# A branch hint at the head of each turn of TensorE's cross-attention loop in a decoder block

## What is computed

```python
x = x + _L0_attn_ref(_layernorm(x), wq, wk, wv, wo)        # causal, 32 heads of 16, 8 key/value heads
x = x + _L0_xattn_ref(_layernorm(x), ctx_4096, mask, Wq, Wk, Wv, Wo, q_norm_w, k_norm_w)
x = x + _L0_ffn_ref(_layernorm(x), gate_w, up_w, down_w, fc1_w, fc2_w, expert_w, ln_gamma, ln_beta)
```

```python
q = _rmsnorm((hidden_states @ Wq.T).reshape(bsz, q_len, H, HD).transpose(0, 2, 1, 3), q_norm_w)
k = _rmsnorm(jnp.repeat(k, GROUPS, axis=1), k_norm_w)
scores = jnp.einsum('bhqd,bhkd->bhqk', q, k) * scale + attention_mask[:, :, :, :kv_len]
probs = jax.nn.softmax(scores.astype(jnp.float32), axis=-1)
out = jnp.einsum('bhqk,bhkd->bhqd', probs, v).transpose(0, 2, 1, 3).reshape(bsz, q_len, H * HD)
return out @ Wo.T
```

## Time and profile before

| what | value |
| --- | --- |
| median of 3 runs | 1723.91 us |
| lowest and highest run | 1723.14 and 1726.42 us |
| the profiled execution | 1727.06 us |
| its span (first to last instruction) | 1725.3 us |
| TensorE matmuls busy | 1644.1 us, 95% |
| TensorE weight loads busy | 1340.6 us, 78% |
| DVE, ACT, POOL busy | 66%, 44%, 38% |
| mean granted TensorE clock | 0.989 of full speed |

### The profile page before, as it was taken

One profiled execution on the slowest core, in us unless ns is written; L12 is line 12 of the kernel. 1 busy time (PEld: TensorE's weight loads), 2 busy tenths in 40 slices (PEclk: granted clock), 3 DMA queues, 4 the chain that ended last, 5 costly groups with the idle time before them and its releaser, 6 DMA issues.

```text
span 1725.3 us, 40966 instructions
## 1 busy us (share of the span) xinstructions
PE 1644.1 (95%) x16856; PEld 1340.6 (78%) x16856; DVE 1141.4 (66%) x1977; ACT 764.2 (44%) x1396; POOL 656.1 (38%) x511
## 2 busy tenths in 40 slices
PE   5899999999999999999978999999999999998998
PEld 5566788887888888788865568888788888786897
DVE  4489767576766666774545877666676766758743
ACT  2576445345354444431225755444454453544321
POOL 3496323234233232461125954243232342324600
PEclk9999999999999999999999999999999999999999
DMA  5110012021020110121111101020120210202100
GB/s 169 62 38 7 20 45 63 2 63 45 20 63 8 57 48 23 50 74 38 54 64 53 31 1 47 17 63 20 44 63 1 63 38 27 69 2 62 31 19 25
DMA packets 26215, 73.04 MB, mean 42 GB/s; under 512 B 3120, under 2 KB 3376, under 8 KB 26032
## 3 DMA queue, kind: packets, MB, share of 16 engines
q1 hardware_dynamic: 26032, 70.22, 13.0%
HBM read 66.01 MB, written 4.19 MB: 41 GB/s over the span
## 4 chain that ended last, share of the span: by engine, by line
PE 64%; issue 13%; POOL 10%; DVE 10%; ACT 2%; DMA 1%; POOLq 0%; SPq 0%; DVEq 0%; ACTq 0%
PE acc L407 10%; PE acc L408 9%; PE acc L409 9%; PE y L407 8%; PE y L409 7%; PE y L408 7%; POOL w_lo L1654 5%; PE quad L672 4%; POOL prob L1667 2%; PE quad L701 2%; PE quad L588 2%; POOL prob L1673 2%; DVE pmax L1247 1%; PE y L685 1%; DVE kv L1347 1%
## 5 line engine op out<-in xcount | busy, mean ns | idle before, releaser
L407 PE MATMUL y<-w_hi 128*128 128x512 f32 x576 | 234.5, 407 | 26.1 <-POOL w_lo L1654 16.7
L1658 POOL TENSOR_TENSOR qkrs<-qkve,mhalf 128x10 f32<-128x10 f32 x64 | 124.9, 1952 | 325.6 <-DVE qkve L1339 325.6
L1667 POOL TENSOR_TENSOR prob<-prob,pmax 128x512 f32<-128x512 f32 x128 | 135.9, 1062 | 274.5 <-DVE pmax L1247 274.0
L407 PE MATMUL acc<-w_hi,xn_hi 128*128 128x512 f32 (+1 forms) x576 | 228.7, 397 | 11.2 <-DVE xn_lo L1188 11.2
L408 PE MATMUL y<-w_lo,w_hi 128*128 128x512 f32 x576 | 226.1, 393 | 0.0
L409 PE MATMUL y<-w_hi,w_lo 128*128 128x512 f32 x576 | 226.1, 393 | 0.0
L408 PE MATMUL acc<-w_lo,xn_hi 128*128 128x512 f32 (+1 forms) x576 | 222.4, 386 | 0.0
L409 PE MATMUL acc<-w_hi,xn_lo 128*128 128x512 f32 (+1 forms) x576 | 220.6, 383 | 0.0
L1264 DVE TENSOR_TENSOR x<-y,x 128x512 f32<-128x512 f32 x144 | 99.3, 690 | 168.2 <-PE y L409 168.2
L1654 POOL TENSOR_TENSOR w_lo<-stage,w_hi 128x1024 fp32r<-128x1024 f32 (+1 forms) x88 | 170.7, 1947 | 89.9 <-ACT w_hi L852 89.9
L1673 POOL TENSOR_TENSOR prob<-prob,prec 128x512 f32<-128x512 f32 x128 | 148.3, 1159 | 137.8 <-DVE prec L1255 137.8
(11 more groups left out here) (129 smaller groups left out, 3773.1 us busy)
## 6 DMA issues: line engine op xcount, KB each, us to landing
stage<-in_w_cross SPq DMA_DIRECT2D x64, 512.0 KB, 3.7
stage<-in_w_cross SPq DMA_DIRECT2D x32, 256.0 KB, 3.3
stage<-in_w_ffn SPq DMA_DIRECT2D x16, 512.0 KB, 3.6
x<-in_x SPq DMA_DIRECT2D x8, 512.0 KB, 3.9
stage<-in_w_self SPq DMA_DIRECT2D x8, 512.0 KB, 4.5
kt<-in_ctx SPq DMA_DIRECT2D x16, 256.0 KB, 2.9
out_x<-x SPq DMA_DIRECT2D x16, 256.0 KB, 2.0
stage<-in_w_self SPq DMA_DIRECT2D x4, 256.0 KB, 3.6
```

The lines of the kernel that those rows point to most:

```text
L407: nc.tensor.matmul(target, l_hi, r_hi, start=first, stop=False)
L1658: return nc.gpsimd.tensor_tensor(target, source, mhalf[:, 0:width], ALU.pow)
L1667: nc.gpsimd.tensor_tensor(pr, pr, spread(pmax[:, buffer, :], 8, SEQ), ALU.subtract).then_inc(s_sub.sem, 1)
```

## The change

The loop of TensorE in `cross_attention` is opened with the option that puts a prefetch hint for the loop's closing branch at the head of the body. The hint is the first instruction of every turn and names the branch that closes the turn. The loops of the other engines are left as they are.

```diff
             def cross_attention(half):
-                with pe.Fori(0, NG - 1) as turn:
+                with nc.Fori(0, NG - 1, engines=bass.OrderedEngineSet([pe.engine]), hint_back_edge=True) as turn:
                     for c in range(CHUNKS):
                         slot(Place(2, half, turn), c)
```

## The result

The median went from 1723.53 us (4 runs, 1720.71 to 1726.42) to 1706.49 us (4 runs, 1702.11 to 1708.24): a ratio of 0.9897, 95% interval 0.9872 to 0.9923. That is 17.0 us less, between 13 and 22. The profiled execution has 1707.25 us with a span of 1705.5. Forecast were 1703.8 us, with a range of 1701.5 to 1712.

A forecast was written before the change was run, and what follows sets the result against it. TensorE was taken as the bound, standing at its loop's closing branch until code was read. From the median 1723.9 us, 12 returns gave -20.2, the hint 0 and leaving the loops 0: 1703.8 us, range 1701.5 to 1712.

The forecast's parts named there:

- The bound and the stall: TensorE bounds; at 12 loop returns it waits for its own code at L720, not POOL: 20.2 us, 1.68 a return.
- (a): Head of each of 14 turns: the added hint instruction costs 0, at most 1.1 us if not covered by queued matmuls.
- (b): At the 12 returns: branches under 3.3 us cost nothing, so the loss of 20.2 us goes.
- (c): Slots around a return: no late data takes the stall's place; DVE's w_lo is ready 1.35 us before the matmul is due.
- (d): Outside the loop: nothing changes, the work there follows TensorE, which arrives earlier by the whole sum.
- leaving the loops 0: At the loops' exits: a term of 0 us in the forecast's sum.
- rival 2: Loop's end: hint comes too late, 1712 us; or it displaces the block behind the loop, exits cost 3.4, 1707.2; together 7%.
- The rule that spoke against it: TensorE's instruction fetch: room for 2048 instructions means no fetch to save, purely sequential prefetch means a useless hint; both 1723.9 us.
- Rivals 1 and 3: At the loop: 1, hint does nothing, 1723.9 us, 9%; 3, hint obeyed at once, one more stop a turn, 1747 us, 5%.
- rival 1: At the returns: the hint does nothing, branches stay at 4.9 us and the time at 1723.9 us; 9%.

The follow-up runs named there:

- written-out run: Kernel before with TensorE's loop written out, 7 groups one after another in each half, no branch: 1702.01 us against 1722.34.
- The runs with the head at 0 and 100: Kernel before, no hint, loop head at a block's start in the first half, 100 instructions in in the second: 1711.93 us against 1724.21.
- two groups a turn and the head at 0: Kernel before with two groups a turn, seventh group behind the loop, hint, both loop heads at a block's start: 1702.14 us against 1724.21.
- The hint last: Changed kernel with the hint moved behind the four slots, directly ahead of the counter's step: 1724.44 us against 1723.57 for the kernel before.
- the first half with two groups: First half of the kernel before with two groups a turn, seventh group behind the loop, and hint: whole kernel 1705.71 us against 1723.57.

## Why the prediction was right, and where it wasn't

*The bound and the stall.* Right. The stop named after POOL wasn't POOL's, the branch at L720 was what held TensorE, and 1.68 us a return was its price on the path. All twelve went, at 20.15 us against 20.2.

*(a) The hint's own price.* Right: 31 ns, 14 times, behind queued matmuls. Slots of 17.19 us show nothing of it.

*(b) The returns.* Right in the sum. The taken branch costs 0.22 us, not DVE's 0.056, which makes no difference below 3.3. The reason behind it was wrong: that TensorE reads its loop afresh in each turn holds for the kernel before, but I carried it over to the changed one, where the hint would only have the head read earlier. 54 packets instead of 162 say that it now reads nothing in turns 2 to 7. That the time came out right in spite of this is luck of a kind: either way the head is there when the branch runs.

The count of blocks was rough too. I spread the queue's bytes over the instructions of all engines and got 65 bytes each; the written-out run shows the packets to be TensorE's (135 packets for its 34526 instructions, 256 each, where all 40544 would make 300). The two come out alike in the kernel before because it reads its loops again. And 1696 left out the register and wait instructions: a turn has 1753, which is 6.85 blocks and not 6.7.

*(c) What is late next.* Right. No wait for DVE's or POOL's data took the stop's place; DVE's w_lo was ready at 282.35, 1.5 us before its matmul.

*(d) and "leaving the loops 0".* Here the prediction failed in a term. The exits, put at 0, cost 3.9 us in the profile: a stop of 2.12 us with the slower clock behind it, and one of 0.61 us with the clock at full speed. In the second profile of the same kernel they cost 7.7. This was in rival 2, as its second case: the hint displaces the block behind the loop, the exits pay like returns, 3.4 us, 1707.2. It came together with the forecast's mechanism, and the median was 1706.5. Among my rivals it stood as an alternative, within a share of 7%; it should have been a term, since a hint that changes what is read at the loop's end changes it in the last turn as well. The first rows to look at were there: behind the exit stands a score block, which uses 256 instructions in 1.6 us. That the median fell inside the forecast's own range (1701.5 to 1707) is in part luck: it lies at the upper end, and when the same kernel was measured again it gained 13.9 us, not 17.0.

*The rule that spoke against it.* I held the Trainium skill's figure (Runtime: NRT & Kernel Launch, "Instruction fetch mechanics": room for 2048 instructions on TensorE) to be contradicted by the 9 packets in a turn. The runs with the head at 0 and 100 show the figure to agree: 7 blocks and one ahead stay, 8 and one ahead don't. What the 9 packets meant was a memory one block short. The section's other sentence, that prefetch is purely sequential, doesn't hold for a hinted branch: with two groups a turn and the head at 0, the branch takes 0.35 us, which it can only do if the head was read out of order ahead of it.

*Rivals 1 and 3.* Neither came in this kernel. The hint last and the first half with two groups have the outcome of rival 1, for other reasons than the one I gave it.

## What to carry to other kernels

Look at the closing branch itself on the engine's sequencer, and at the packets of the instruction queue, before believing the releaser that a wait names: a row of 5 us there, or a loop whose later turns still read code, is a stall that no data explains. Count in blocks of 16.4 KB where the loop's body lies. If it can lie in one block less than the memory holds, place its head at a block's start: that took away 20 us here with no hint and no cost at the exit. If it can't, give the hint well before the last block (17 us ahead of the branch was enough here, 0.2 us wasn't), place the head so that the branch stands well inside its block, and put slow work (few instructions, long matmuls) behind the exit.

## What the runs showed that I had not expected

- Kept code. A loop of 1753 TensorE instructions a turn runs from the engine's memory, with no packet in five turns, and one block more makes it read 9 packets in every turn.
- A branch back costs 0.21 to 0.22 us where the code is kept and 0.35 to 0.38 where the head was read ahead of it, against 4.6 to 5.3 where it was not there.
- Where the loop falls in its blocks decides by itself: the same source without a hint gave 0.21 us branches in one half and 5.0 in the other.
- A stop for code of 2.12 us was followed by matmuls at half pace (0.43 us apart against 0.23, granted clock 0.50), so that 3.80 us were lost by the next product; one of 0.61 us left the clock at 1.00 and lost 0.94 us.
- The cost of the exits varies between executions of one kernel: the second half's stop was 0.61 us in one profile and 2.50 in the other.
